# TensorE's order in a slot: the query projection moved in front of the key projection

## The reference

```python
xn = (x - mean) / sqrt(var + 1e-5)
q, k, v = split(xn @ Wqkv.T + bqkv)          # 16 heads of 32
scores = mask + 32 ** -0.5 * einsum('bnd,bmd->bnm', q, k)
attention = einsum('bnm,bmd->bnd', softmax(scores), v) @ Wproj.T + bproj
linear = fp8(xn) @ fp8(Wffn).T + bffn        # products rounded to float16
out = x + attention + linear
```

## Time and profile before

| | us |
|---|---|
| median of 3 runs | 1607.78 (1607.31 to 1608.79) |
| the profiled execution's own time | 1606.56 |
| span of the profile | 1604.8 |
| mean granted TensorE clock over the span | 0.984 |

### The profile page before, as it was taken

One profiled execution on the slowest core, in us unless ns is written; L12 is line 12 of the kernel. 1 busy time (PEld: TensorE's weight loads), 2 busy tenths in 40 slices (PEclk: granted clock), 3 DMA queues, 4 the chain that ended last, 5 costly groups with the idle time before them and its releaser, 6 DMA issues.

```text
span 1604.8 us, 25152 instructions
## 1 busy us (share of the span) xinstructions
PE 1508.1 (94%) x6913; PEld 676.9 (42%) x6913; DVE 1442.9 (90%) x1188; ACT 1059.3 (66%) x2010; POOL 1381.5 (86%) x1046
## 2 busy tenths in 40 slices
PE   4998999999999999999999999999999999999945
PEld 3443444444444344444444444443444444444412
DVE  7389999989999899989999899998999899999892
ACT  5675676666766676766767667675776767667532
POOL 1288989888998989889898898989899898989885
PEclk7999999999999999999999999999999999999988
DMA  6344444545454554544445444454545444454333
GB/s 198 74 99 96 108 119 123 119 105 124 117 125 111 112 125 114 128 106 118 124 111 131 105 119 123 114 128 106 122 121 118 112 117 122 120 118 111 92 76 85
DMA packets 366532, 184.30 MB, mean 115 GB/s; under 512 B 314160, under 2 KB 314160, under 8 KB 366384
## 3 DMA queue, kind: packets, MB, share of 16 engines
q1 hardware_dynamic: 366384, 182.53, 46.8%
HBM read 73.41 MB, written 33.55 MB: 67 GB/s over the span
## 4 chain that ended last, share of the span: by engine, by line
POOL 38%; issue 34%; DVE 14%; PE 4%; POOLq 1%; DVEq 1%; DMA 0%; SPq 0%; ACT 0%; ACTq 0%
POOL prod_pv L391 18%; DVE prod_qk L720 7%; POOL xs L445 6%; POOL x L428 4%; DVE scores L725 4%; POOL o L417 3%; POOL prod_qk L439 2%; POOL rstd L423 2%; POOL probs L402 2%; POOL shifted L411 2%; DVE stats L749 1%; PE k_ps L602 1%; PE v_ps L602 1%; POOLq L79 1%; PE proj_ps L602 1%
## 5 line engine op out<-in xcount | busy, mean ns | idle before, releaser
L391 POOL TENSOR_TENSOR prod_pv<-kv,probs 128x2048 f32<-128x2048 f32 x192 | 699.2, 3642 | 14.5 <-POOL probs L402 7.7
L758 DVE TENSOR_REDUCE o_nat<-prod_pv 128x512 f32<-128x2048 f32 (+1 forms) x128 | 429.1, 3353 | 59.0 <-POOL prod_pv L391 44.6
L725 DVE TENSOR_REDUCE scores<-prod_qk 128x64 f32<-128x2048 f32 x192 | 439.3, 2288 | 15.6 <-DVE prod_qk L720 9.4
L720 DVE TENSOR_TENSOR prod_qk<-q_ps,kv 128x1536 f32<-128x1536 f32 (+1 forms) x192 | 397.9, 2072 | 2.7 <-ACT kv L557 2.7
L602 PE MATMUL k_ps<-wqkv_hi,xT 128*128 128x512 f16 x1024 | 328.5, 382 | 38.5 <-DMA xT<-x 38.5
L602 PE MATMUL proj_ps<-wproj_hi,oT 128*128 128x512 f16 x1032 | 333.0, 384 | 0.0
L602 PE MATMUL v_ps<-wqkv_hi,xT 128*128 128x512 f16 x1024 | 325.4, 379 | 0.0
L602 PE MATMUL q_ps<-wqkv_hi,xT 128*128 128x512 f16 x1024 | 325.4, 379 | 0.0
L566 ACT ACTIVATE kv<-v_ps 128x512 f32<-128x512 f32 x128 | 142.3, 1112 | 172.4 <-PE v_ps L602 171.1
L557 ACT ACTIVATE kv<-k_ps 128x512 f32<-128x512 f32 x128 | 76.4, 597 | 197.8 <-PE k_ps L602 191.5
L602 PE MATMUL proj_ps<-wproj_lo,oT 128*128 128x512 f16 x516 | 200.1, 388 | 0.0
(11 more groups left out here) (117 smaller groups left out, 1851.1 us busy)
## 6 DMA issues: line engine op xcount, KB each, us to landing
xn<-in_L_attn_x SPq DMA_DIRECT2D x128, 256.0 KB, 2.9
xs<-in_L_attn_x SPq DMA_DIRECT2D x128, 256.0 KB, 2.9
out<-xs SPq DMA_DIRECT2D x128, 256.0 KB, 2.2
xT<-x SPq DMA_TRANSPOSE x256, 3.0
kv<-in_L_attn_Wqkv SPq DMA_DIRECT2D x3, 1024.0 KB, 10.0
oT<-o SPq DMA_TRANSPOSE x128, 3.1
kv<-in_L_ffn_weight SPq DMA_DIRECT2D x1, 1024.0 KB, 5.7
kv<-in_L_attn_Wproj SPq DMA_DIRECT2D x1, 1024.0 KB, 14.2
```

What stands on the lines that cost most here:

```text
L391: nc.gpsimd.tensor_tensor(o, v, p, ALU.mult).then_inc(pv_multiplied, 1)
L720: nc.vector.tensor_tensor(prod_qk[:, 1:1 + m0 + 4 - m1, :], qb, k, ALU.mult).then_inc(qk_multiplied, 1)
L725: nc.vector.tensor_reduce(scores[:, n % 2, :, m0:m0 + 4].rearrange("p h m -> p m h"), prod_qk[:, row:row + 4, :].rearrange("p m (h d) -> p ...
L758: nc.vector.tensor_reduce(o_nat[:, n % 2, :], prod_pv[:, place:place + units, :].rearrange("p q (c m) -> p c q m", m=4), AX_XY, ALU.add).t ...
```

## The change

The block of the queries moves, with its wait, from the end of TensorE's slot to the place between linear and keys. In slot j it is still the queries of tile j-5 and the keys and values of tile j-4. No other engine's program is touched.

```diff
                     last.then_inc(lin_summed, 1)
+                if live(i, j, L_Q):
+                    n = j - L_Q
+                    after(pe, q_preset, tile_count(i, n))
+                    split_products(q_ps[n % 4], xT[:, n % XT, :, :], wqkv_hi, wqkv_lo, 0,
+                                   first=False).then_inc(q_summed, 1)
                 if live(i, j, L_KV):
                     n = j - L_KV
                     t = xT[:, n % XT, :, :]
...
                     split_products(k_ps, t, wqkv_hi, wqkv_lo, C, first=False).then_inc(k_summed, 1)
                     after(pe, v_kept, tile_count(i, n - 1))
                     split_products(v_ps, t, wqkv_hi, wqkv_lo, 2 * C).then_inc(v_summed, 1)
-                if live(i, j, L_Q):
-                    n = j - L_Q
-                    after(pe, q_preset, tile_count(i, n))
-                    split_products(q_ps[n % 4], xT[:, n % XT, :, :], wqkv_hi, wqkv_lo, 0,
-                                   first=False).then_inc(q_summed, 1)
```

## The result

The changed kernel takes 1627.28 us (median of 4 runs, 1626.4 to 1627.75) beside 1607.99 us of the kernel before in the same comparison: a ratio of 1.0119, 95% interval 1.0102 to 1.0137. The forecast, 1621.7 us, had the sign and the range, but the loss is 19.3 us, not 13.9. The profiled execution took 1627.75 us, its span is 1626.0 and its mean granted clock 0.986. One run of the kernel before and one of the experiment with the early preset took over 5600 us; these two are left out of all medians here. A trace shows one execution: the trace of the kernel before is of one that took 1606.56 us, 1.4 us less than the median beside it, so the two spans differ by 21.2 us where the medians differ by 19.3.

A forecast was written before the change was run, and what follows sets the result against it. VectorE and GpSimd, with issue gaps, were taken as the bound, not TensorE. The fill's delay of 13.9 us, steady state and back-edges 0, gave 1620.5 from the profiled execution, 1621.7 us from the median; range 1616 to 1627, wider 1614 to 1629.

The forecast's parts named there:

- Key waits stay: Steady state: TensorE's stall in front of the keys remains, since values to keys keeps the same 29 matmuls; gain 0.
- the key waits really go: Rival: the 38.5 us of TensorE's waits for xT before the keys vanish, 1583 us at best; chance 0.07.
- (a): Fill, slot 5: first queries move before keys 1 without a wait; everything hanging on keys and values comes 2.59 us later.
- (b): Fill, slots 6 to 9: queries wait for ACT's preset behind the value copy, 1.88 us in each slot, +7.52.
- (c): Fill, slot 10: ACT now has an exponential too, so the preset ends later and TensorE stalls, +1.99 us.
- (d): Fill, slot 11: ACT also copies the first query, preset ends at 94.94 with TensorE ready at 92.58, +2.46 us.
- The rival on the clock: Fill, slots 6 to 11: stalls drop TensorE's clock for one or two groups each, 15 to 30 us later; chance 0.06.
- What reaches DVE: Slot 12: DVE's row sum waits for ACT's late exponential, leaving DVE 13.9 us late; this goes on into the run.
- the slack: POOL's slots 15 to 17: 0.3 us left of 2.69; rival says overrun or back-edges cost 2 to 6 us more, chance 0.09.
- Back-edges: Loop's 6 back-edges: queries wait about 0.5 us for the preset, hidden before xT arrives; 0, at most 3.0 us.
- the signs that I had named: Signs of being wrong: key waits gone, clock below 1 at 55 to 140 us, query waits inside loop, changing shift.

## Why the prediction was right in kind and short by 5 us

*Key waits stay, keys and values are the fixed point: right.* 32.0 us of key waits are left of 38.5, and most of the missing part is slot 16's. That wait was a slack of the fill; losing it won nothing. The rival "the key waits really go" is refuted. The Trainium skill, page "Perfetto Trace Analysis", section "Optimization Strategies", names as the goal a matmul engine that is kept as busy as possible, and says to speed up the engines that it waits for. The runs bear out the second half. With the holes filled by useless work PE was busy 87.26 us of the 92 instead of 75.31, and the kernel still took 1625.3 us; with ACT's preset earlier it was busy 90.76 us, and the kernel took 1614.4.

*(a) Slot 5, +2.59: right.* The shift went from 0.9 to 3.5.

*(b) Slots 6 to 9, 1.88 each: right.* 3.5 to 10.9 in four slots is 1.85 each, and the beat is 9.61 us, forecast 9.65. The waits themselves are shown with 1.67 us and, from slot 11 on, 2.25, not 1.9 and 2.5: a matmul's shown end lies some 0.17 us behind the place where the next could start. The hand-over from preset to matmul was 0.06 us (59.08 - 58.32 - 0.70), not 0.10.

*(c) Slot 10, +1.99: right,* 1.9 measured.

*(d) Slot 11, +2.46: mis-sized, 4.1 measured.* The preset part was right, but the clock fell there for about 3.5 us and the group took 1.7 us longer. The rival on the clock had one or two groups in each of six slots and 15 to 30 us; it was one group. The clock rival was thus right that the clock can fall in this fill and wrong in size. Five holes of 1.67 to 1.77 us in a beat of 9.6 us passed at a full clock, the sixth, of 2.25 us, did not, and the seventh and eighth, of 2.25 and 2.27 us, did. The Trainium skill, page "TensorE: Matmul & The Clock Gate", Part 1, says that activity releases the throttle. The trace with the holes filled agrees, with a clock of 1.00, but so had one of five with the holes left open.

*What reaches DVE, 13.9: right once the clock is taken out.* The row sum of slot 12 was due at 116.31 and came at 118.71, a shift of 16.3 against the earlier trace rows; less 0.8 of start and 1.7 of clock that is 13.8. From there on the shift of the fill stayed constant: no slack gave it back. POOL's wait in slot 17 kept 0.42 us where I had 0.3, so the slack was not overrun.

*Back-edges, taken as 0 with at most 3.0: the step that failed, 4.1 measured.* I had asked what the queries would wait for at a back-edge (0.5 us forecast, 0.98 seen) and not what else comes earlier: PE's own branch, and with it its code fetch. The work between two slots' keys had kept its length, but the place of the branch in it had not. The growth from round to round, which I had named as what would prove me wrong, is this term. Two more of the signs that I had named came too: query waits inside the loop (5.7 us), and a granted clock below 1 between 55 and 140 us. The measured 1627.3 lies just outside the forecast's own range, 1616 to 1627, and inside the wider one, 1614 to 1629.

The sum of what was measured: 13.8 of the fill as DVE saw it, 1.7 of clock, 4.1 of back-edges; that is 19.6. With the 0.8 of start and the 0.8 of the tail it makes the 21.2 us between the two traces; between the medians there are 19.3.

*What is shown and what is not.* Shown: the fill costs by the late preset; the price of the one fall of the clock; that the growth lies at the back-edges, in front of DVE's first work, and belongs to the new order together with PE's hardware loop. Supported by four traces of five: that the clock falls in slot 11 because of the holes. Supported, not isolated: that it is the meeting of PE's fetch with those of DVE and ACT. In the eight traces with PE's loop, DVE's gaps sum to 25.1 to 26.3 us where PE's second packet comes 0.2 to 2.0 us behind DVE's branch (five traces), and to 20.9 to 21.6 where it comes 3 us or more behind it (three); no run moved a fetch and nothing else. POOL's branch moves as well, from 5.0 to 5.7 us ahead of DVE's, but it lies 5.3 to 6.0 ahead with TensorE written out in the new order, where the gaps are small. Open: the 1.5 us of the kernels with TensorE written out, the 2.3 us by which the shift shrinks without loops, and the loss of the tail.

## What to carry to other kernels

A wait on the busiest engine that moves with another engine's pace can't be scheduled away; ask which instruction holds the releaser before reordering the waiter, and keep an operand's preset at least one group of work ahead of its reader, counted in the fill as well, where nothing else lies between. Follow a late start until every engine is late alike: what is lost before that point is lost once, what is lost at a loop's edge is lost every round. And when an order changes, look at where it puts each engine's branch, and at every boundary between the old order and the new.

## What the runs showed of the hardware

- Between its branch at a back-edge of the hardware loop and its next work DVE stands 3.4 to 4.0 us in the kernel before and 3.8 to 4.7 in the changed one, with bodies of 16 slots; writing out the loop (six back-edges) won 19.0 us of 1608. The edge costs more in the traces where PE's second packet of code comes 0.2 to 2.0 us behind DVE's branch (25.1 to 26.3 us in all, against 20.9 to 21.6); that the one causes the other is not isolated.
- The length of the last hole does not settle whether the granted clock falls. In the changed kernel's fill one hole of 2.25 us was followed by 3.4 us at the 1.2 GHz level, which cost one group of 12 matmuls 1.7 us, and the next two, of 2.25 and 2.27 us, were not; another trace with the same holes kept the full clock.
- A kernel paced by DVE and POOL lost 24 us when the keys and values, and ACT with them, were made 2.6 us late in one slot of 16, at the edge. The fall of the clock that follows in each round (3.4 or 6.8 us) is part of that price, so it is not the price of the late tile alone.
